# Attention kernel: GpSimd normalises x in a pass that subtracts the mean and passes that multiply by the inverse deviation

## The reference, cut to what matters

```
def _layernorm(x, axis=-1, eps=1e-05):
    m = jnp.mean(x, axis=axis, keepdims=True)
    v = jnp.var(x, axis=axis, keepdims=True)
    return (x - m) / jnp.sqrt(v + eps)
...
    h = h + _L0_attn_ref(_layernorm(h, axis=-1), L0_attn_Wq, L0_attn_Wk, L0_attn_Wv, L0_attn_Wo)
    h = h + _L0_ffn_ref(_layernorm(h, axis=-1), L0_ffn_w, L0_ffn_b)
```

## Time and profile before

| | |
|---|---|
| median of 3 runs | 1489.23 us (1484.79 to 1493.75) |
| the profiled execution's own time | 1493.45 us |
| its span (first to last instruction) | 1491.6 us |
| mean granted TensorE clock | 0.983 |
| busy: PE, DVE, POOL, ACT | 1428.2, 1160.9, 921.2, 734.1 us |

### The profile page before, as it was taken

How to read it: one execution, slowest core, us unless ns; L and a number is a source line. 1 busy time by engine, 2 the same in 40 slices (tenths; PEclk the granted TensorE clock), 3 DMA queues, 4 the chain that set the end, 5 groups by cost and what they waited for, 6 DMA issues and landing times.

```text
span 1491.6 us, 34063 instructions
## 1 busy us (share of the span) xinstructions
PE 1428.2 (96%) x10442; PEld 1109.5 (74%) x10442; DVE 1160.9 (78%) x2285; ACT 734.1 (49%) x2673; POOL 921.2 (62%) x958
## 2 busy tenths in 40 slices
PE   5999888999999999999999999889999999999997
PEld 3999866777777777777777777676677777777774
DVE  7888678789999999999999998787765655656555
ACT  6897566576767676676767676562000000000000
POOL 5796156576767767676767767445555556455552
PEclk8999999999999999999999999999999999999998
DMA  9356666677767777777767776867434344343442
GB/s 236 102 142 152 191 142 164 181 191 204 202 200 205 201 210 194 209 194 203 200 196 206 198 206 189 259 207 200 149 113 148 116 130 134 112 145 116 133 113 60
DMA packets 264458, 255.60 MB, mean 171 GB/s; under 512 B 73329, under 2 KB 201586, under 8 KB 264402
## 3 DMA queue, kind: packets, MB, share of 16 engines
q1 hardware_dynamic: 257586, 233.87, 56.4%
q10 hardware_dynamic: 6816, 21.04, 4.7%
HBM read 138.26 MB, written 106.57 MB: 164 GB/s over the span
## 4 chain that ended last, share of the span: by engine, by line
PE 79%; DVE 7%; POOL 6%; DMA 3%; issue 2%; SPq 2%; ACT 1%; ACTq 0%; DVEq 0%; POOLq 0%
PE att_ps L1098 33%; PE ffn_o L1747 22%; PE ffn_y L1839 7%; PE att_ps L1141 4%; PE att_ps L1153 4%; POOL yb L358 3%; PE att_ps L1130 2%; PE att_ps L1122 2%; POOL yb L364 2%; PE mix_ps L447 1%; DMA p_blocks<-pB 1%; SPq L876 1%; PE att_ps L1109 1%; DMA xqT<-xq 1%; DVE m L641 1%
## 5 line engine op out<-in xcount | busy, mean ns | idle before, releaser
L1223 ACT ACTIVATE pr<-sm,ml 128x128 f32<-128x128 f32 x1024 | 399.1, 393 | 164.6 <-DVE ml L1401 163.3
L979 POOL TENSOR_TENSOR pr<-pr,ri 128x512 f32<-128x512 f32 x256 | 266.9, 1043 | 206.9 <-DVE ri L1408 199.8
L1098 PE MATMUL att_ps<-w_lo,xT_hi 128*128 128x512 f32 x776 | 319.9, 412 | 0.0
L1098 PE MATMUL att_ps<-w_hi,xT_hi 128*128 128x512 f32 x776 | 312.5, 403 | 3.9 <-DVE xT_lo L1349 3.1
L1098 PE MATMUL att_ps<-w_hi,xT_lo 128*128 128x512 f32 x776 | 307.6, 396 | 0.0
L1801 ACT CAST cT_hi<-ctx_in 128x512 fp32r<-128x512 f32 x64 | 36.4, 616 | 363.1 <-PE ffn_o L1747 350.8
L1747 PE MATMUL ffn_o<-wo_hi,cT_hi 128*128 128x512 f32 x528 | 211.8, 401 | 2.3 <-DVE wo_lo L1790 1.7
L1392 DVE TENSOR_TENSOR sm<-att_ps,cst 128x512 f32<-128x512 f32 x256 | 170.0, 664 | 51.9 <-PE att_ps L1141 51.9
L1747 PE MATMUL ffn_o<-wo_hi,cT_lo 128*128 128x512 f32 x528 | 205.7, 390 | 0.0
L1747 PE MATMUL ffn_o<-wo_lo,cT_hi 128*128 128x512 f32 x528 | 205.4, 389 | 0.0
L1223 ACT ACTIVATION_READ_ACCUMULATOR pr<-sm,ml 128x1 f32 x1024 | 193.4, 189 | 0.0
(11 more groups left out here) (212 smaller groups left out, 2340.7 us busy)
## 6 DMA issues: line engine op xcount, KB each, us to landing
pT<-p_blocks SPq DMA_DIRECT2D x256, 256.0 KB, 2.9
p_blocks<-pB SPq DMA_DIRECT2D x512, 64.0 KB, 2.0
h_rows<-ho SPq DMA_DIRECT2D x64, 256.0 KB, 3.8
ctx_turned<-ctxo SPq DMA_DIRECT2D x64, 256.0 KB, 3.6
h_in<-h_rows SPq DMA_DIRECT2D x32, 512.0 KB, 3.7
out_dram<-yo SPq DMA_DIRECT2D x32, 512.0 KB, 2.7
ctx_in<-ctx_turned SPq DMA_DIRECT2D x30, 512.0 KB, 3.3
hbuf<-h_rows ACTq DMA_DIRECT2D x29, 512.0 KB, 4.7
```

The costliest lines, as they stand in the source:

```text
L979: G.tensor_tensor(pr[:, g % 4], pr[:, g % 4], ri[:, g % 2, :].unsqueeze(2).to_broadcast([P, GQ, P]), ALU.mult).then_inc(p_ready, 1)
L1098: mm = nc.tensor.matmul(bank[:], x_part[:, t[1], e, tok:tok + P], w_part[blk][:, e, :], start=(r == 0), stop=(r == EC * 3 - 1))
L1223: a = nc.scalar.activation(pr[:, g % 4, q, :], sm[:, g % 2, q, :], ACT.Exp, bias=ml[:, b[1], 0, h:h + 1], accum_out=ml[:, b[1], 1, h:h + 1])
```

## The change

POOL's normalisation of a tile is 2 instructions before, each on 512 columns, with two scalars in memory (mean and inverse deviation). After, it is 3: `centre` on all 1024 columns (less the mean, times the constant 1), from `hbuf` to `xn`, and then `normalise` in place on each half (times the inverse deviation, plus the constant 0). `centre` stands in s = 3, where the first half was; the first half's `normalise` moves to s = 4, behind `rope_sum`; the second half's stays in s = 5. A semaphore `x_centred`, counted by POOL and waited for by POOL, orders the passes. The waits for `rstd_ready` and `x_turned` keep their place in the loop.

```diff
+        def centre(n):
+            if at(n, 0):
+                pool.wait_ge(rstd_ready, nth(n) + 1)
+                pool.wait_ge(x_turned, 2 * nth(n))
+            G.tensor_scalar(xn[:], hbuf[:, n[1], :], mv[:, 0:1], 1.0, ALU.subtract, ALU.mult
+                            ).then_inc(x_centred, 1)
+
         def normalise(n, r):
             if at(n, 0) and r == 0:
-                pool.wait_ge(rstd_ready, nth(n) + 1)
-                pool.wait_ge(x_turned, 2 * nth(n))
+                pool.wait_ge(x_centred, 1)
             cols = slice(r * BK, (r + 1) * BK)
-            G.tensor_scalar(xn[:, cols], hbuf[:, n[1], cols], mv[:, 0:1], rstd[:], ALU.subtract, ALU.mult
-                            ).then_inc(xn_ready, 1)
+            G.tensor_scalar(xn[:, cols], xn[:, cols], rstd[:], 0.0, ALU.mult, ALU.add).then_inc(xn_ready, 1)
...
                 inverse_deviation(n)
+                centre(n)
                 normalise(n, 0)
...
                 if s == 3 and has_rows(n) and not last_rows(n):
-                    normalise(n, 0)
+                    centre(n)
+                if s == 4 and has_rows(n) and not last_rows(n):
+                    pool.wait_ge(x_centred, number(n) + 1)
                 if s == 4 and has_rows(t):
                     rope_sum(t, 0)
+                if s == 4 and has_rows(n) and not last_rows(n):
+                    normalise(n, 0)
                 if s == 4 and exists(c, NB):
                     save_ctx(c, 0)
```

More of the change, by code:

```diff
@@ L721, in attention_stage @@
     w_rounded_pool = sem("w_rounded_pool")
+    x_centred = sem("x_centred")
     quantised = sem("quantised")
```

## The result

The changed kernel takes 1518.14 us (median of 4 runs, 1512.19 to 1524.23), the kernel before 1490.25 us (4 runs, 1484.79 to 1493.75): ratio 1.0191, 95% interval 1.0164 to 1.0217. The forecast was 1489 us, within 0.5% of before, so it missed by 29 us, well outside its range. Rival A, "the subtracting pass is slow", is what happened; it stood there with 1523 to 1532 us for a pass of 4.17 us and a chance of 0.11.

A forecast was written before the change was run, and what follows sets the result against it. PE, busy 96% of the span, was taken as the bound. With 0 from the loop and 0 from the written-out iterations, the profiled 1493.45 us stayed; lying 4.2 us above the median, it gave 1489, range 1483 to 1499.

The forecast's parts named there:

- Rival A: POOL's centre pass takes up to 4.17 us, making PE's key transpose and DVE's transpose late: 1523 to 1532 us; chance 0.11.
- I take 1.14 us, because form and size agree: POOL's centre pass on 1024 columns priced like L970 (mult and add), at 1.14 us, with 4.17 us as upper end.
- a factor of two for the second scalar: POOL's L965: its second scalar in memory costs most of a factor of two; the operations may cost something too.
- The Trainium skill's line rate: POOL near 1.03 cycles per element with one tensor input: 0.88 us a tile before, 1.76 after; same conclusion on PE.
- the two halves: POOL's two multiplying passes on 512 columns, in s = 4 and s = 5: 0.67 us each, 1.33 for both.
- that PE doesn't wait for `xn` itself: Moved half in s = 4: `xn` half 0 ready two microseconds later, but PE has 4 us to spare.
- It decides from a pass of about 2.09 + 1.0 = 3.1 us; with less than that it is hidden.: Threshold for a slow centre pass: the rotary sum has about 1.0 us of slack before PE's transpose of the keys.
- DVE's slack as cover in step 5: `normalise_p` of s = 5 ends later, but DVE takes it 1.0 us after that; without cover, 10 us.
- rival D: POOL's wait on its own semaphore, or the shifted order, costs PE up to 10 us: 1499 us; chance 0.05.
- with a centre pass of 1.14 us nothing moves: In the loop, POOL's saved time becomes a longer wait for DVE's reciprocals; the iteration stays at 24 us, gain 0.
- at most 7.4 us of idle time is left: Loop, 260 to 900 us: PE busy 632.57 of 640 us, so any gain there is at most 0.5%.
- Rival C: An engine off the path, such as DVE, quickens while POOL is quiet and closes PE's last gaps: 1485 us; chance 0.06.

The follow-up runs named there:

- e1: The kernel before with 42 extra POOL instructions ahead of it, 14 forms of tensor_scalar, three of each, timed singly; 1569.30 us, a total that says nothing.
- e4: The changed kernel with the centre pass on 768 columns in place of 1024, the second half multiplied straight from `hbuf`; 1496.30 us, ratio 1.004.
- e2: The kernel before with only the order changed: the first half's old pass moved to s = 4, behind the rotary sum; 1503.96 us, ratio 1.008.
- e5: The changed kernel with nothing moved, only quick operations: centre as times -1 plus mean, normalise as times inverse deviation times -1; 1489.08 us, ratio 0.999.
- e9: The kernel before with DVE taking the lower part of x's first half ahead of the transpose of probabilities in step 7; 1480.38 us, ratio 0.9921.
- e3: The changed kernel with the centre pass in halves, in steps 3 and 5, and the second half's multiplication in step 6; 1494.41 us, ratio 1.0036.
- e7: The changed kernel with the first half's multiplication moved from step 4 to step 5, ahead of the second half's; 1501.48 us, ratio 1.0074.
- e6: The changed kernel with the rotary sum of the keys ahead of `normalise_p` in step 4; 1531.10 us, ratio 1.028.

## Why the prediction was wrong, by its own steps

- **Failed: "I take 1.14 us, because form and size agree".** This is the step, the price of the centre pass. The pass took 3.71 us. The prediction had asked the right question, operands or operations, and had the rows for the answer: by its own figures L358 (two scalars, mult and add) costs 2.1 ns a column and L965 (two scalars, subtract and mult) 3.7. That pair differs in the operations alone, and sizes aside it says that subtract is dear. I then read a factor of two for the second scalar out of a comparison of 128 columns with 1024, where the fixed part decides: e1 gives 0.45 us on 128 columns and 0.77 on 512 for the same form, so 0.32 us for 384 columns, 0.83 ns a column, and a fixed part of about 0.34 us, not the 0.194 that I had borrowed from a copy. The second scalar costs 0.07 us, not most of a factor of two.
- **The Trainium skill's line rate** ("GPSIMD Engine Reference", sections 3.1 and 4.1): the quick pairs are near it (1.12 to 1.16 us on 1024 columns against an estimate of 0.88 by the page), and subtract (3.70) and one operation alone (2.84) contradict it, though both have one tensor input. So the prediction's 1.76 us a tile by the page is far from the 5.10 measured.
- **Right: the two halves** at 0.67 us (0.69), and that PE doesn't wait for `xn` itself.
- **Right in mechanism: rival A.** It named both waits, 1.1 to 1.4 us a tile; measured 1.1. It had 31 tiles where 25 tiles' worth was paid, and a pass of 4.17 in place of 3.71. By its own working a pass of 3.71 us costs some 0.6 us at the keys, and 0.67 was measured; the other half of the 1.1 came in front of the second transpose of x, so that its total per tile comes close is partly luck.
- **Partly wrong: "It decides from a pass of about 2.09 + 1.0 = 3.1 us; with less than that it is hidden."** That is right for the transpose of the keys (e4, 2.86 us, shows no wait there), but e4 is 0.3 us an iteration slower than before: the moved half adds itself behind the centre pass and DVE's transpose of step 6 has no pause behind it. The prediction had treated DVE's slack as cover in step 5 and hadn't carried the lateness on to step 6; it named the effect as rival D; e2 shows it at 0.8% for a pass of 2.08 us in step 4, and with the quick centre pass in front of it (e5) the moved half costs nothing that shows.
- **Right: with a centre pass of 1.14 us nothing moves.** e5 has this pass, and its time is within 0.3% of before by its interval.
- **Wrong: "at most 7.4 us of idle time is left", as the ceiling of a gain.** In the 24 iterations compared under e9 PE idled 3.3 us, and 8.6 us were gained. The sum of PE's idle time was no ceiling, since the four transposes behind the gap took longer than without it. Rival C itself, that a quieter POOL lets DVE run faster, didn't happen: in e5 POOL is busy 53 us less and DVE's busy time is 1161.2 us in place of 1160.9.

What stays open: the 0.36% of e3, the two ends of e9, and why a pair with subtract, or a single operation, costs POOL more; the runs show that it does, not what it does in them.

## What to carry to other kernels

Price an instruction from a row with the same operations, and compare two rows only at the same size; where no such row exists and the two ends differ by a factor of over three, the chance of the dear end is not one in nine. On an engine that runs without a pause between two deadlines, ask for the length of the work between these deadlines and follow a delay until it meets a pause; nearly the same work of POOL, 5.1 to 5.4 us a tile, cost 28, 12 or 6 us (the changed kernel, e7, e3), by the place of its parts. A small gap of PE that returns in every iteration can be worth more than its length; here it was 0.35 us for a gap of 0.11 to 0.16.

## What the runs showed of the hardware that I had not expected

- POOL's tensor_scalar in f32 on 128x1024: 1.12 to 1.16 us for mult-mult, add-mult and mult-add, 3.70 us for a pair with subtract in either place, 2.84 us for a single operation, be it subtract or mult. So at this size and type a subtraction is better written as times -1 plus the scalar, and a lone multiplication as a pair.
- Behind a PE gap of 0.11 to 0.16 us four transposes of 128x128 took 0.63 us, and 0.44 without the gap.
- POOL's wait for its own last instruction left it idle for 0.25 us in e6 (between the centre pass and the rotary sum), for 0.16 us in e3, and for about 0.1 us between the passes of e1, where nothing else stood between them; without such a wait the next instruction starts some 0.03 us before the end of the one before it.
